# A gated cross-attention layer on one core: group loads first in SyncE's turn, rows of maxima sent by GpSimd, maxima eight groups of tiles ahead

## The chip, the cores and the metric

One core of one Trainium2 chip. The metric is device time in microseconds (us) of one execution of the whole program, as a median over runs.

## The reference, cut to what matters

Everything is float32. Four sequences of 512 tokens, width 256, 16 heads of 16.

```python
q = split_heads(layernorm(x) @ Wq.T + bq);  k, v = the same from ctx_1024
scores = einsum('bhqd,bhkd->bhqk', q, k) / 4
attn   = softmax(scores, axis=-1)
x = x + tanh(g_xattn) * (merge_heads(attn @ v) @ Wo.T + bo)
# then: a mixture of 8 experts, 2 per token, and a shared gated MLP
h = layernorm(x);  x = x + tanh(g_ffn) * (moe(h) + shared(h))
```

## The kernel before

The program has three stages. In the first, up to about 57 us, x is normalised, Q and K are projected, and each is split into a high and a low part (rows of the float32r format that TensorE multiplies), which are stored to DRAM (`q_parts`, `k_parts`). The second, from about 57 to about 335 us, is the attention loop. The third is the output projection, the router, the shared MLP and the experts.

The attention loop runs over `GROUPS` = 16 groups of `G` = 4 heads of one sequence, each in four steps `kt` over tiles of 128 keys. A step has four score products (L1608), one for each head, whose results ScalarE turns into exponentials (L806), and the products with the values of the step before (L1487), which ScalarE copies out of PSUM (L792). GpSimd adds the four steps' sums (`add_part`, L671). The transposed scores have the keys on the partitions, so the maximum over the keys can't be taken there. The kernel computes the scores a second time, with the queries on the partitions (`scores_for_max`, L1374), ahead of time, and VectorE reduces them (`two_max`, L929). The negated maxima of a group then travel: GpSimd splits them in two parts (`split_max`, L579 and L581), VectorE transposes them (`turn_max`, L937), GpSimd copies them into rows (`max_rows`, L591), and a transfer puts the rows under the Q rows of the group (`load_max`, L397). They are two more rows of the contraction of L1608, so that the maximum is subtracted in the product.

How far the maxima run ahead is `EARLY`: 28 tiles are done in the first stage by `early_max`, one at a time (L915), and `smax_schedule` then gives each step of the loop the four tiles numbered `4 * i + EARLY // TB + kt`, in fours. With 28 that is the last four tiles of group i+1 at `kt` = 0 and the first twelve of group i+2 at `kt` = 1 to 3. TensorE reaches each step's tiles after its first two scores.

`QS` and `KST` hold the Q and K rows of `NG` = 4 groups. `load_group(i)` (L387, L390) brings a group's rows from DRAM in twelve transfers of 64 KB. It may start when the scores of group i-4 are done (`st_done`).

Three more chains run in the loop. `load_sums` (L402) takes the softmax denominators of a finished group, `scale_of` (VectorE, L977) inverts them, `store_scale` (L406) and `load_scale` (L413) spread them by way of DRAM. `pack_out` (L665) moves the four heads' results from `OT` into `CTX`. `scale_context` (GpSimd, L622) multiplies two groups' results with their scales; it runs in odd turns from 5 on. `load_scale(i)` waits for `scale_context` of the pair before, since it overwrites its scales.

The order of each engine's work is written out by hand, and every queue runs in order. SyncE's turn i of the loop was `load_max(i+1)`, `load_sums(i-1)`, `store_scale(i-2)`, `load_scale(i-3)`, `load_group(i+3)`. GpSimd's turn was `split_max(i+1)`, `max_rows(i+1)`, `add_part(i-1, 3)`, `pack_out(i-1)`, `bias_x` (in the first six turns), `add_part(i, 1)`, `scale_context`, `add_part(i, 2)`. On VectorE `turn_max(i+1)` stands after the first reduction of step `kt` = 1 and `scale_of(i-2)` after that of `kt` = 2. In the last two groups a list of tail jobs (output projections, layer norm, router) is placed between the steps of TensorE and VectorE; `scale_of` of the last group comes in the last turn, ahead of the job of its step.

The last two groups do not go through `pack_out` (`TURNED` = 14): TensorE transposes their sums (`out_transpose`, L1497), which waits for GpSimd's last `add_part`.

Of the kernel before, what the change touches and what calls it, by code (L numbers as in the profile page):

```python
# [5 lines left out]
P = 128  # L6
# [3 lines left out]
F32 = mybir.dt.float32  # L10
# [5 lines left out]
def flamingo_layer(nc, x, ctxT, g_xattn, g_ffn, WqT, bq, WkT, bk, WvT, bv, WoT, bo,  # L16
# [3 lines left out]
    DK = D // H  # L20
    T = B * S
    NT = T // P
    TB = S // P
# [6 lines left out]
    G = 4  # L30
# [36 lines left out]
    with ExitStack() as stack:  # L67
# [6 lines left out]
        def sems(name, n):  # L74
            return [sem(f"{name}{i}") for i in range(n)]
# [145 lines left out]
        summed = sem("summed")  # L221
        st_done, exp_done, pv_done, sums_out = sems("st_done", 2), sem("exp_done"), sem("pv_done"), sem("sums_out")
        ot_t, rden_ready, ctx_ready = sem("ot_t"), sem("rden_ready"), sem("ctx_ready")
        ctx_in, den_in, scale_out = sems("ctx_in", 2), sems("den_in", 2), sems("scale_out", 2)
        scale_ready, scale_in, ctx_scaled = sem("scale_ready"), sems("scale_in", 2), sem("ctx_scaled")

        ct_t, wo_done, x1_ready = (sem(n) for n in ("ct_t", "wo_done", "x1_ready"))
# [34 lines left out]
            return range(UP * m, UP * (m + 1))  # L262

        STEPS = GROUPS * TB
        EARLY = 7 * G
        EARLY_J = ((0, 0, 0, 0), (0, 0, 0, 0), (2, 2, 4, 4), (4, 4, 4, 4))

        def max_tile(n):

# [76 lines left out]
        def times(i):  # L346
            return 16 * (i // 2 + 1)

        @block.sync
        def _(sp):  # L350
            sp.dma_start(CT[:, 0, :, :], ctxT[:, 0:S].rearrange("(c p) n -> p c n", p=P)).then_inc(ct_in[0], 16)
# [39 lines left out]
                                 k_scr[b, K_PART[t], rows, :].rearrange("(h r d) n -> r d h n", r=2, d=DK)[r])\  # L391
                      .then_inc(ld_group[g], 16)

            def load_max(i):
                sp.wait_ge(m_ready, TB * (i + 1))
                for part in range(2):
                    sp.dma_start(QS[i % NG][KS + part:P:HALF, :, :].bitcast(F32).rearrange("p h n -> p (h n)"),  # L397
                                 mparts[G * TB * part:G * TB * (part + 1), i % 2, :]).then_inc(m_in[i % 2], 16)

            def load_sums(i):  # L400
                sp.wait_ge(summed, (TB - 1) * (i + 1))
                sp.dma_start(DENS[:, i % 2, :], OT[i % 2][DK:P:P // G, :].rearrange("j (q n) -> j q n", n=G * TB)).then_inc(den_in[i % 2], 16)  # L402
# [28 lines left out]
            load_group(1)  # L431
            store_parts(2)
            load_group(2)
            load_max(0)
            load_group(3)
            store_parts(3)
            for i in range(GROUPS):
                if i + 1 < GROUPS:
                    load_max(i + 1)
                if 0 <= i - 1 < TURNED:  # L440
                    load_sums(i - 1)
                if 0 <= i - 2 < TURNED:
                    store_scale(i - 2)
                if 0 <= i - 3 < TURNED:
                    load_scale(i - 3)
                if i and (i + 3) % NG == 0 and i + 3 < GROUPS:
                    parts_stored((i + 3) // NG)
                if 0 < i and i + 3 < GROUPS:
                    load_group(i + 3)
                if i == GROUPS - NG + 1:  # L450
                    for t_, src in ((wgate, gate_w), (wup, up_w), (wdown, down_w)):
                        sp.dma_start(t_[:, :, :], src.rearrange("(c p) n -> p c n", p=P)).then_inc(w_in["shared"], 16)
                    sp.wait_ge(wr_zero, 1)
                    sp.dma_start(wr[:, :, 0:E], w_router.rearrange("(c p) n -> p c n", p=P)).then_inc(w_in["router"], 16)
                if i == 4:
                    parts_stored(B - 1)
                for e in EXPERTS_AT.get(i, ()):
                    load_expert(e)
                if i == GROUPS - 1:
                    sp.wait_ge(zero_ready, 3)  # L460
                    sp.dma_start(slot_x[E * CAP:ROWS, :].rearrange("(n p) d -> p n d", p=P),
                                 ZERO[:, :].unsqueeze(1).to_broadcast([P, SPARE, DT])).then_inc(zero_out, 16)
# [69 lines left out]
        def _(pool):  # L532
# [51 lines left out]
            def max_rows(i):  # L584

                pool.wait_ge(turned_max, i + 1)
                if i >= 2:
                    pool.wait_ge(m_in[i % 2], 32 * (i // 2))
                for k in range(TB):
                    at = slice(32 * k, 32 * (k + 1))  # L590
                    nc.gpsimd.tensor_copy(mparts[:, i % 2, at], mturned[at, i % 2, :]).then_inc(m_ready, 1)  # L591
                pool.wait_ge(m_ready, TB * (i + 1))

            pool.wait_ge(kones, NG)
            pool.wait_ge(w_in["small"], 64)
# [21 lines left out]
            def scale_context(n):  # L617

                for h in range(2):
                    pool.wait_ge(ctx_in[h], 16 * G * (n + 1))  # L620
                    pool.wait_ge(scale_in[h], 16 * (n + 1))
                nc.gpsimd.tensor_tensor(CTX[:, n, :], CTX[:, n, :], SCALES, ALU.mult).then_inc(ctx_scaled, 1)  # L622

# [36 lines left out]
            def pack_out(i):  # L660

                pool.wait_ge(summed, (TB - 1) * (i + 1))
                for j in range(G):
                    at = G * DK * (i % 2) + DK * j
                    pool.dma_start(CTX[at:at + DK, i // 2, :], OT[i % 2][P // G * j:P // G * j + DK, :]).then_inc(ctx_in[i % 2], 16)  # L665

            def add_part(i, kt):

# [1 line left out]
                pool.wait_ge(summed, (TB - 1) * i + kt - 1)  # L670
                nc.gpsimd.tensor_tensor(OT[i % 2], OT[i % 2], PART[kt - 1], ALU.add).then_inc(summed, 1)  # L671

            bias_x(range(4))
            for i in range(TURNED + 1):
                split_max(i + 1)
                max_rows(i + 1)
                if i:
                    add_part(i - 1, 3)
                    pack_out(i - 1)
                if i < 6:  # L680
                    bias_x(range(4 + 2 * i, 6 + 2 * i))
                add_part(i, 1)
                if i >= 5 and i % 2:
                    scale_context((i - 5) // 2)
                if i < TURNED:
                    add_part(i, 2)
# [26 lines left out]
        def _(act):  # L713
# [69 lines left out]
            def sums_copy(n):  # L783

                i, kt = divmod(n, TB)
                act.wait_ge(pv_done, n + 1)
                if kt == 0 and 2 <= i < TURNED + 2:
                    act.wait_ge(ctx_in[i % 2], G * times(i - 2))
                    act.wait_ge(den_in[i % 2], times(i - 2))
                if kt and i:  # L790
                    act.wait_ge(summed, (TB - 1) * (i - 1) + kt)
                nc.scalar.copy(PART[kt - 1] if kt else OT[i % 2], PS[:, ring_bank("sums", n), :]).then_inc(sums_out, 1)  # L792
# [97 lines left out]
        def _(dve):  # L890
# [304 lines left out]
            for i in range(GROUPS):  # L1195
                for kt in range(TB):
                    t = smax_schedule(i, kt)
                    for h in range(2):
                        if t is not None:
                            two_max(TB * t + 2 * h)  # L1200
                        if kt == 1 and h == 0 and i + 1 < GROUPS:
                            turn_max(i + 1)
                        if kt == 2 and h == 0 and 0 <= i - 2 < TURNED:
                            scale_of(i - 2)
                        if kt == 1 and h == 0 and i > TURNED:
                            denominators(i - 1)
                        if kt == 1 and h == 1 and i > TURNED:
                            head_out(i - 1)
                    tail(TB * i + kt - TAIL)
# [645 lines left out]
```

## Time and profile before

| what | us |
|---|---|
| median of 3 runs | 553.59 (552.21 to 557.13) |
| the profiled execution | 550.5 |
| its span in the profile | 548.6 |
| TensorE busy in it | 460.8 (84% of the span) |
| VectorE, ScalarE, GpSimd busy | 314.8, 269.8, 223.9 |
| mean granted TensorE clock | 0.903 of full speed |

Busy TensorE counts weight loads and low clock as they come, so a busy share of 84% does not say how near to its peak the engine is. The loop and the stage behind it have different limits, and what a change in the loop is worth is read from the waits inside it. In a line of the timeline the bracket at the end tells how long the engine sat idle ahead of it and what ended that.

### The profile page before, as it was taken

To read this page: it belongs to the slowest core of one execution; us is meant where nothing else is said; L and a number is where in the kernel's file an instruction comes from. 1 tells how busy PE (TensorE), PEld (TensorE's weight loads), DVE (VectorE), ACT (ScalarE), POOL (GpSimd) and SP (SyncE) were. 2 spreads that over 40 slices of the span, in tenths; PEclk is the share of its full clock that TensorE was granted. 3 is DMA by queue.
4 is the path that set the end of the run, shared out by engine and by line. 5 is a ranking of instruction groups with operands and counts; after the bars stand their busy time and mean duration, and the time that the engine had idled before them with its cause. 6 is when DMAs were issued, how large, how long until landed. Compare 5 with 4: busy or idle time off the path is not lost.

```text
span 548.6 us, 8362 instructions
## 1 busy us (share of the span) xinstructions
PE 460.8 (84%) x2294; PEld 232.4 (42%) x2294; DVE 314.8 (57%) x719; ACT 269.8 (49%) x564; POOL 223.9 (41%) x345
## 2 busy tenths in 40 slices
PE   9999897768836766586359997899799999999997
PEld 7554432322312222132123453546555555555555
DVE  2958667657625644565357476574556655662375
ACT  2454487767626735565366643110246666662100
POOL 5445526656613633444145525767012332322100
PEclk9999889888768867878687998999899999999999
DMA  8699602233033223321351807713222322221651
GB/s 270 238 267 244 201 21 70 69 81 76 17 67 80 50 45 66 79 59 34 67 119 41 252 3 209 232 70 111 63 59 89 86 88 81 87 88 39 228 193 58
DMA packets 45500, 58.93 MB, mean 107 GB/s; under 512 B 12496, under 2 KB 25680, under 8 KB 45456
## 3 DMA queue, kind: packets, MB, share of 16 engines
q1 hardware_dynamic: 38864, 46.05, 30.5%
q0 software_dynamic: 4960, 10.53, 5.8%
q10 hardware_dynamic: 1632, 1.84, 1.0%
q8 instruction: 19, 0.31, 0.2%
q14 instruction: 25, 0.20, 0.1%
HBM read 36.35 MB, written 19.81 MB: 102 GB/s over the span
## 4 chain that ended last, share of the span: by engine, by line
PE 59%; issue 10%; DMA 9%; SPq 8%; DVE 6%; POOL 6%; ACT 1%; another core or an unknown queue 1%; ACTq 0%; POOLq 0%; DVEq 0%
PE PS L1652 10%; PE PS L1762 8%; PE PS L1487 6%; DMA QK<-k_parts 6%; PE PS L1665 5%; PE PS L1374 5%; PE PS L1608 4%; PE PS L1781 4%; SPq L387 4%; SPq L390 3%; PE PS L1427 3%; DVE nmax L929 3%; PE PS L1757 3%; PE PS L1534 2%; POOL R L671 2%
## 5 line engine op out<-in xcount | busy, mean ns | idle before, releaser
L929 DVE TENSOR_REDUCE nmax<-PS 128x2 f32<-128x1024 f32 x114 | 135.2, 1212 | 105.7 <-PE PS L1374 105.4
L806 ACT ACTIVATE R<-PS 128x512 f32<-128x512 f32 x256 | 135.6, 624 | 85.0 <-PE PS L1608 83.6
L1374 PE MATMUL PS<-QK 48*128 48x512 f32 x256 | 71.6, 511 | 69.0 <-DMA QK<-k_parts 68.5
L1608 PE MATMUL PS<-QK 50*128 50x512 f32 x256 | 89.2, 516 | 2.0 <-ACT R L723 1.2
L1487 PE MATMUL PS<-R 128*32 128x512 f32 x512 | 82.0, 717 | 2.8 <-ACT R L806 1.6
L1374 PEld LDWEIGHTS PS<-QK 48*128 48x128 f32 x256 | 37.1, 231 | 88.6 <-DMA QK<-k_parts 73.0
L671 POOL TENSOR_TENSOR R<-R 128x512 f32<-128x512 f32 x48 | 61.8, 1287 | 31.2 <-ACT R L792 29.4
L1608 PEld LDWEIGHTS PS<-QK 50*128 50x128 f32 x256 | 42.1, 218 | 71.5 <-issue 32.6
L708 POOL DMA_INDIRECT token_y<-R,dest x34 | 32.7, 961 | 92.1 <-DVE R L1257 90.7
L591 POOL COPY mparts<-mturned 32x32 f32<-32x32 f32 x64 | 12.8, 200 | 93.6 <-DVE mturned L937 90.8
L792 ACT COPY R<-PS 128x512 f32<-128x512 f32 x64 | 38.5, 602 | 22.1 <-PE PS L1487 21.9
L1762 PE MATMUL PS<-R 128*128 x100 | 47.3, 595 | 0.2 <-ACT R L874 0.2
L821 ACT ACTIVATE R<-PS 128x512 f32<-128x512 f32 x16 | 9.6, 597 | 71.3 <-PE PS L1652 50.0
L1652 PE MATMUL PS<-R,wup 128*128 128x512 f32 x64 | 33.6, 648 | 2.3 <-issue 2.3
L629 POOL DMA_INDIRECT slot_x<-CH,pos x32 | 31.1, 971 | 10.6 <-issue 8.4
L1295 DVE TENSOR_TENSOR R<-R,PS 128x256 f32<-128x256 f32 x34 | 14.3, 421 | 32.5 <-issue 20.0
L1652 PE MATMUL PS<-R,wgate 128*128 128x512 f32 x64 | 30.6, 595 | 1.4 <-issue 1.4
L665 POOL DMA_DIRECT2D CH<-R x56 | 27.8, 502 | 4.3 <-POOL R L671 4.2
L1665 PE MATMUL PS<-wdown,R 128*128 128x256 f32 x128 | 28.9, 380 | 0.0
L871 ACT ACTIVATE R<-PS 128x256 f32<-128x256 f32 x34 | 13.0, 383 | 30.0 <-PE PS L1762 26.2
L1665 PEld LDWEIGHTS PS<-wdown,R 128*128 128x128 f32 x128 | 24.2, 192 | 4.9 <-issue 2.0
L1781 PE MATMUL PS<-fc,R 128*128 x100 | 25.6, 380 | 0.0
(181 smaller groups left out, 628.7 us busy)
## 6 DMA issues: line engine op xcount, KB each, us to landing
QK<-q_parts SPq DMA_DIRECT2D x96, 64.0 KB, 3.2
QK<-k_parts SPq DMA_DIRECT2D x96, 64.0 KB, 3.3
k_parts<-R SPq DMA_DIRECT2D x8, 512.0 KB, 3.9
q_parts<-R SPq DMA_DIRECT2D x8, 512.0 KB, 4.7
R<-in_fc_w_dram SPq DMA_DIRECT2D x16, 256.0 KB
R<-token_y SPq DMA_DIRECT2D x4, 1024.0 KB, 9.0
R<-slot_x SPq DMA_DIRECT2D x25, 129.0 KB
fc<-in_fc_w_dram SPq DMA_DIRECT2D x16, 128.0 KB
```

Of the source, the lines that this page charges most:

```text
L671: nc.gpsimd.tensor_tensor(OT[i % 2], OT[i % 2], PART[kt - 1], ALU.add).then_inc(summed, 1)
L708: nc.gpsimd.indirect_dma_start(token_y, bass.IndirectOffsetOnAxis(ap=dest[:, j:j + 1], axis=0), YE[:, j % UN, :], None).then_inc(y_out[j % ...
L792: nc.scalar.copy(PART[kt - 1] if kt else OT[i % 2], PS[:, ring_bank("sums", n), :]).then_inc(sums_out, 1)
L806: nc.scalar.activation(PT[:, kt, j, :], PS[:, ring_bank("score", TB * i + kt, j), :], ACT.Exp).then_inc(exp_done, 1)
L929: nc.vector.tensor_reduce(nmax[:, i % 2, at:G * TB:G * TB // 2], PS[:, smax_bank(n):smax_bank(n) + 2, :], AX.X, ALU.max, negate=True).then ...
L1374: mm(PS[:, smax_bank(n), :], QS[g][at, h, qt * P:(qt + 1) * P], KST[g][at, h, :], start=True, stop=True).then_inc(smax_done[n % 2], 1)
L1487: last = mm(PS[32 * j:32 * j + VW, ring_bank("sums", n), :], VA[:, b * TB + kt, (g * G + j) * VS:(g * G + j) * VS + VW], PT[:, kt, j, :], ...
L1608: mm(PS[:, ring_bank("score", TB * i + kt, j), :], KST[g][at, h, kt * P:(kt + 1) * P], QS[g][at, h, :], start=True, stop=True).then_inc(st ...
L1652: last = mm(PS[:, gu_bank(n, k), :], w[:, d, c * P:(c + 1) * P], H2T[:, d, b * S:(b + 1) * S], start=(d == 0), stop=(d == DC - 1))
L1665: last = mm(PS[:, down_bank(b, t), half * D:(half + 1) * D], HS[:, b % 2, c, t * P:(t + 1) * P], wdown[:, c, :], start=(c == 0 and half == ...
L1762: last = mm(PS[:, 1 + u, :], XGT[:, u, c * P:(c + 1) * P], fc1[:, c, e, :], start=(c == 0), stop=(c == DC - 1))
L1781: last = mm(PS[:, 5 + u, 0:D], HET[:, u, c * P:(c + 1) * P], fc2[:, c, e, :], start=(c == 0), stop=(c == IE // P - 1))
```

## The change

SyncE's turn begins with `load_group(i+3)`. `load_max` is gone from SyncE; its two transfers are issued by GpSimd at the end of `max_rows`. `EARLY` is 32, so that the tiles of a step belong to group i+2 as a whole, and the first stage does four more single maxima. `turn_max` moves from `kt` = 1 to `kt` = 0, `scale_of` from 2 to 1. Two of the four transfers of `pack_out` go to SyncE (`pack_heads`), with a semaphore for each half. On GpSimd `add_part(i-1, 3)` comes ahead of `max_rows(i+1)`, and the first `bias_x` moves behind it.

```diff
-        EARLY = 7 * G
-        EARLY_J = ((0, 0, 0, 0), (0, 0, 0, 0), (2, 2, 4, 4), (4, 4, 4, 4))
+        EARLY = 8 * G
+        EARLY_J = ((0, 0, 0, 0), (0, 0, 0, 0), (2, 2, 4, 4), (4, 4, 6, 6))
...
+        def pack_heads(queue, i, heads, done):
+
+            for j in heads:
+                at = G * DK * (i % 2) + DK * j
+                queue.dma_start(CTX[at:at + DK, i // 2, :], OT[i % 2][P // G * j:P // G * j + DK, :]).then_inc(done[i % 2], 16)
...
-            load_max(0)
             load_group(3)
             store_parts(3)
             for i in range(GROUPS):
-                if i + 1 < GROUPS:
-                    load_max(i + 1)
+                if i and (i + 3) % NG == 0 and i + 3 < GROUPS:
+                    parts_stored((i + 3) // NG)
+                if 0 < i and i + 3 < GROUPS:
+                    load_group(i + 3)
                 if 0 <= i - 1 < TURNED:
                     load_sums(i - 1)
+                    pack_heads(sp, i - 1, (2, 3), ctx_high)
                 if 0 <= i - 2 < TURNED:
                     store_scale(i - 2)
                 if 0 <= i - 3 < TURNED:
                     load_scale(i - 3)
-                if i and (i + 3) % NG == 0 and i + 3 < GROUPS:
-                    parts_stored((i + 3) // NG)
-                if 0 < i and i + 3 < GROUPS:
-                    load_group(i + 3)
...
                 pool.wait_ge(turned_max, i + 1)
                 if i >= 2:
+                    pool.wait_ge(summed, (TB - 1) * (i - 1))
                     pool.wait_ge(m_in[i % 2], 32 * (i // 2))
                 for k in range(TB):
                     at = slice(32 * k, 32 * (k + 1))
                     nc.gpsimd.tensor_copy(mparts[:, i % 2, at], mturned[at, i % 2, :]).then_inc(m_ready, 1)
                 pool.wait_ge(m_ready, TB * (i + 1))
+                for part in range(2):
+                    pool.dma_start(QS[i % NG][KS + part:P:HALF, :, :].bitcast(F32).rearrange("p h n -> p (h n)"),
+                                 mparts[G * TB * part:G * TB * (part + 1), i % 2, :]).then_inc(m_in[i % 2], 16)
...
             def pack_out(i):
 
                 pool.wait_ge(summed, (TB - 1) * (i + 1))
-                for j in range(G):
-                    at = G * DK * (i % 2) + DK * j
-                    pool.dma_start(CTX[at:at + DK, i // 2, :], OT[i % 2][P // G * j:P // G * j + DK, :]).then_inc(ctx_in[i % 2], 16)
+                pack_heads(pool, i, (0, 1), ctx_low)
...
-            bias_x(range(4))
             for i in range(TURNED + 1):
                 split_max(i + 1)
+                if i:
+                    add_part(i - 1, 3)
                 max_rows(i + 1)
                 if i:
-                    add_part(i - 1, 3)
                     pack_out(i - 1)
+                else:
+                    bias_x(range(4))
...
-                        if kt == 1 and h == 0 and i + 1 < GROUPS:
+                        if kt == 0 and h == 0 and i + 1 < GROUPS:
                             turn_max(i + 1)
-                        if kt == 2 and h == 0 and 0 <= i - 2 < TURNED:
+                        if kt == 1 and h == 0 and 0 <= i - 2 < TURNED:
                             scale_of(i - 2)
```

## Rows read from the trace of the kernel before

**Rows 1.** The list of waits of TensorE: in total, times, longest us.

```profile
PE PS L1374 <- DMA QK<-k_parts: 68.5, 12, 8.8
```

**Rows 2.** Busy time in windows: group 1, and a cycle with the wait.

```profile
core 0: us, PE busy (x) PEld busy (x) DVE busy (x) ACT busy (x) POOL busy (x), PEclk, DMA share, GB/s
76.90:86.90 10.00, 9.97 (x70) 3.85 (x66) 9.49 (x10) 9.96 (x21) 6.28 (x13) 1.00 0.09 23
...
223.40:243.70 20.30, 12.33 (x68) 4.59 (x64) 9.66 (x11) 10.30 (x21) 8.04 (x14) 0.75 0.28 64
```

**Rows 3.** Timeline of TensorE: starts of groups 2, 10 and 14, and one wait.

```profile
86.88 0.50 PE L1608 MATMUL PS<-QK 50*128 50x512 f32 x2
...
223.45 0.50 PE L1608 MATMUL PS<-QK 50*128 50x512 f32 x2
...
234.40 0.79 PE L1374 MATMUL PS<-QK 48*128 48x512 f32 x2 [7.87 <-DMA QK<-k_parts]
...
298.36 0.50 PE L1608 MATMUL PS<-QK 50*128 50x512 f32 x2
```

**Rows 4.** The list of waits of SyncE's queue: in total, times, longest us.

```profile
SPq L397 <- POOL mparts L591: 89.8, 14, 14.3
```

**Rows 5.** Timeline of SyncE's queue, one cycle: start, us, what it issues.

```profile
217.69 1.11 SPq L397 DMA_DIRECT2D QK<-mparts  x2
219.06 0.60 SPq L402 DMA_DIRECT2D DENS<-R  x1
220.56 0.34 SPq L406 DMA_DIRECT2D o_scales<-SCALE  x1
224.49 0.56 SPq L413 DMA_DIRECT2D w_v<-o_scales  x1
225.28 0.31 SPq L387 DMA_DIRECT2D QK<-q_parts  x1
...
230.30 0.42 SPq L390 DMA_DIRECT2D QK<-k_parts  x1
```

**Rows 6.** The chain that ended last: start, us, what, at that cycle's last load.

```profile
230.30 4.06 DMA QK<-k_parts
```

**Rows 7.** Timeline of GpSimd, the first bias_x, and the cycle of rows 5.

```profile
58.89 2.78 POOL L658 TENSOR_TENSOR X<-X,tg_bo 128x256 f32<-128x256 f32 x4
...
216.69 0.98 POOL L591 COPY mparts<-mturned 32x32 f32<-32x32 f32 x4 [6.45 <-DVE mturned L937]
...
219.33 1.96 POOL L665 DMA_DIRECT2D CH<-R  x4 [0.30 <-POOL R L671]
...
223.15 1.27 POOL L622 TENSOR_TENSOR CH<-CH,w_v 128x512 f32<-128x512 f32 x1
224.39 1.29 POOL L671 TENSOR_TENSOR R<-R 128x512 f32<-128x512 f32 x1
226.75 0.20 POOL L579 CAST nmax_parts<-nmax 128x16 fp32r<-128x16 f32 x1 [1.07 <-DVE nmax L929]
227.03 0.22 POOL L581 TENSOR_TENSOR nmax_parts<-nmax,nmax_parts 128x16 f32<-128x16 f32 x1
```

**Rows 8.** Timeline of ScalarE: the copy of group 9's last sums.

```profile
226.17 0.58 ACT L792 COPY R<-PS 128x512 f32<-128x512 f32 x1
```

**Rows 9.** Timeline of VectorE: four reductions without a gap, and a transposition that waited.

```profile
221.95 4.74 DVE L929 TENSOR_REDUCE nmax<-PS 128x2 f32<-128x1024 f32 x4 [0.34 <-PE PS L1374]
...
302.18 0.21 DVE L937 STREAM_TRANSPOSE mturned<-nmax_parts 128x32 f32<-128x32 f32 x1 [0.59 <-POOL nmax_parts L581]
```

**Rows 10.** Line L665, GpSimd's 56 context transfers of 32 KB: issue to landing.

```profile
DMA to landing us min/median/max: 1.8/2.0/4.4
```

**Rows 11.** Timeline of VectorE: four single maxima at the end of the first stage.

```profile
56.73 2.48 DVE L915 TENSOR_REDUCE nmax<-PS 128x1 f32<-128x512 f32 x4 [0.56 <-PE PS L1374]
```

**Rows 12.** The last group: VectorE's timeline, the chain that ended last, TensorE's timeline.

```profile
326.93 0.25 DVE L977 RECIPROCAL SCALE<-DENS 128x16 f32<-128x16 f32 x1
...
328.78 6.50 DMA w_v<-o_scales
...
339.37 0.66 PE L1497 MATMUL PS<-ident,R 128*128 128x128 f32 x4 [3.25 <-POOL R L671]
```

More of the change, by code:

```diff
@@ L223, in flamingo_layer @@
         ot_t, rden_ready, ctx_ready = sem("ot_t"), sem("rden_ready"), sem("ctx_ready")
-        ctx_in, den_in, scale_out = sems("ctx_in", 2), sems("den_in", 2), sems("scale_out", 2)
+        ctx_low, ctx_high = sems("ctx_low", 2), sems("ctx_high", 2)
+        den_in, scale_out = sems("den_in", 2), sems("scale_out", 2)
         scale_ready, scale_in, ctx_scaled = sem("scale_ready"), sems("scale_in", 2), sem("ctx_scaled")
@@ L392, in load_group @@
                       .then_inc(ld_group[g], 16)
[L394 to L398, printed above, removed]
             def load_sums(i):
@@ L619, in scale_context @@
                 for h in range(2):
-                    pool.wait_ge(ctx_in[h], 16 * G * (n + 1))
+                    pool.wait_ge(ctx_low[h], 16 * 2 * (n + 1))
+                    pool.wait_ge(ctx_high[h], 16 * 2 * (n + 1))
                     pool.wait_ge(scale_in[h], 16 * (n + 1))
@@ L787, in sums_copy @@
                 if kt == 0 and 2 <= i < TURNED + 2:
-                    act.wait_ge(ctx_in[i % 2], G * times(i - 2))
+                    act.wait_ge(ctx_low[i % 2], 2 * times(i - 2))
+                    act.wait_ge(ctx_high[i % 2], 2 * times(i - 2))
                     act.wait_ge(den_in[i % 2], times(i - 2))
```

## The prediction

> **What bounds the kernel now.** I read the list of waits first, then busy time by stage, then the timelines of the engines over two cycles of the attention loop. The loop runs over 16 groups of 4 heads, each in four steps kt. The list of waits says that TensorE's scores for the maxima (L1374) waited 68.5 us, in 12 pieces, for the transfers that load a group's Q and K rows [rows 1]. That is the largest wait of any engine for a transfer in this loop, and TensorE is the engine on which the others wait. The windows show what a cycle would be without it: group 1, from 76.9 to 86.9, takes 10.0 us with TensorE busy 9.97, ScalarE 9.96 and VectorE 9.49, at full granted clock; a cycle with the wait takes 20.3 us at a granted clock of 0.75 [rows 2]. The TensorE rows place the wait: it falls in step kt = 1 (group 10, begun at 223.45: 7.87 us), because there the scores for the maxima reach group i+2, whose rows land only then. Group 2 begins at 86.88 and group 14 at 298.36: 12 cycles in 211.5 us, 17.6 us each [rows 3].
>
> Why the rows land late stands in SyncE's order. It waited 89.8 us for the rows of maxima that GpSimd makes [rows 4]. In one cycle its queue sends those at 217.69, the denominators at 219.06, the scales at 224.49, and only then starts the twelve loads, 225.28 to 230.30 [rows 5]. The last one lands 4.06 us after its issue [rows 6]. So a load takes 9.1 us from first issue to landing, and it starts up to 1.8 us after group 10 began, or several us into a group in the other cycles, while its space has been free since the last scores of the group before.
>
> **The change part by part.** I call the start of a group T and one cycle P, and take the offsets from group 10 (T = 223.45).
>
> *Group loads first, and rows of maxima off SyncE.* SyncE's turn i now starts with load_group(i+3), which needs only the last scores of group i-1 (about T - 0.7) and a free queue. Its other work of a turn is 12 x 0.47 = 5.6 us of load issues, 0.6 for the denominators, 0.56 for the scales, 0.34 to store them, and now two context transfers, no row shows them on SyncE, at 0.42 each like a load's issue (0.60 like the denominators' at most): 8.0 us, 8.3 at most [rows 5], below any P considered. In a turn with even i the queue is late: the turn before ended with load_scale, which waits for scale_context on GpSimd. That ran at 223.15 [rows 7], and load_scale followed at 224.49 [rows 5]; this dependence stays. So in every second cycle the loads still start at T + 1.8 and land at T + 10.9. In the other they start near T - 0.5 and land at T + 8.6.
>
> *Maxima 32 tiles ahead instead of 28.* Group i+2 is now needed at kt = 0, a step (2.5 us) earlier: at T + P + 0.35, after two scores. Against T + 10.9 that asks for P of about 10.55 in late cycles and nothing in the others. The 68.5 us wait goes, and with it the low clock that follows each piece of it.
>
> *turn_max one step earlier.* What is late next is VectorE. turn_max waits for split_max on GpSimd. Today the last reduction of a group ends a step later, and split_max starts at 226.75, with GpSimd idle before it [rows 7]. In the changed order that reduction ends about 2.4 us earlier, near T + 0.9, but GpSimd is in add_part(i-1, 2) until 224.39 + 1.29 = T + 2.2 [rows 7], since it starts those adds only behind ScalarE's copy of the sums. The split takes 0.5, so it is done at T + 2.8, while VectorE, after one more reduction, is there at T + 2.1. It waits 0.7 us per group. A wait of this kind has a row in group 14: 0.59 us [rows 9]. VectorE's own work is 8 reductions at 4.74/4 = 1.185, a transposition of 0.21 and a reciprocal of 0.25: 9.9 us [rows 9, 12]. Records overlap at their ends: group 1, which has no reciprocal, shows 9.49 busy [rows 2], so I take 9.75. With the wait it is 10.45. The reductions free the banks that TensorE fills, so this sets P in the cycles whose loads come early, and the loads set 10.55 in the others. I take P = 10.5.
>
> *Rows of maxima sent by GpSimd.* The chain is: values of (i-1, 3) at kt = 0, ScalarE's copy from 226.17 [rows 8], add_part(i-1, 3) at T + 3.4 to 4.7, four copies to 5.7 (they take 0.98), two DMA issues. No row shows GpSimd sending these; its context transfers cost 1.96 for four [rows 7], so two cost 1.0 and are out at T + 7.0. They land in 1.8, 2.0 or 4.4 us (least, median, most) [rows 10]. I take 2.0: ready at T + 9.0, 1.5 us before the next group wants them. At 4.4 it would be T + 11.4, and that would be P. GpSimd's turn is 7.5 us of work (three adds 3.9, split 0.5, copies 1.0, four issues 2.0), 8.8 with scale_context, 1.4 more in the first six turns for bias_x (2.78 for four, [rows 7]): it fits. A rule of the Trainium skill speaks against this part: in SBUF — State Buffer, § Who interferes with whom, and the warning on the "DVE blocks DMA" trap, a DMA from GpSimd's queue is starved while VectorE runs in a 2-port mode, and SyncE's queue is immune. The same section says that tensor_reduce has no such mode on trn2. By the rule alone the sum would gain nothing from this part and could lose; with its exception it stands as it is. Nearly all VectorE work in the loop is that reduction.
>
> *Half the context transfers on SyncE* takes 1.0 us of issue from GpSimd and costs 0.9 on SyncE, in slack on both. They are needed only two groups later.
>
> *Prologue.* Four more single maxima (2.48/4 = 0.62 each, [rows 11]) go ahead of group 0, on a VectorE that is nearly full there: at most 2.5 us. The first scores move by 2.0. bias_x(0..3), 2.8 us of GpSimd, moves behind the first rows of maxima, where GpSimd was idle: nothing. Bounds 0 to 3.
>
> *Tail.* scale_of(13) ran at 326.93, behind the VectorE work of a tail step; one step earlier it runs near 322. The scales landed 6.5 us after 328.78, GpSimd waited for them before scale_context, its last adds came after that, and TensorE waited 3.25 us for these at 339.37 [rows 12]. With the scales 5 us earlier, the adds follow ScalarE's copies: the 3.2 us go. Bounds 0 and 3.2.
>
> **The sum.** 12 cycles at 10.5 are 126.0 against 211.5: -85.5. Group 1 gets VectorE's wait too: +0.5. Prologue +2.0, tail -3.2. Together -86.2. The profiled execution took 550.5 us, so 464.3. It lies 3.1 under the median of the runs, 553.6; I predict 467 for the median.
>
> **The rivals.**
>
> *A. Rows of maxima late.* GpSimd's issues cost more than 0.5, or the transfers land in 4.4 us beside the group loads. For: a 4.4 occurs, and its chain now ends 1.5 us before the need. Against: median 2.0. P becomes 11.4 to 12, 12 cycles: +11 to +18, 478 to 485.
>
> *B. The load wait stays in part.* SyncE in the late turns is held beyond T + 1.8, as scale_context now stands behind more GpSimd work and the loads share the engines with more transfers. P about 13 in a mean: +30, 497. If every cycle kept half of its excess over 10.5 it would be near 14, and 509. For: the late cycle has no slack. Against: the same dependence gives T + 1.8 today, and in slack.
>
> *C. Not faster.* The new ring, from a group's first values over copy, add, rows and GpSimd's transfers to the next group's start, sets P. From T + 7.0 it must take 10.6 us to land to give back 17.6. The largest landing is 4.4. Time then 553.
>
> *D. Better than the sum.* VectorE's wait is absorbed and loads land sooner: P = 10.0, the pace of group 1, and no prologue cost: 459. I count it to the likeliest case.
>
> *E. The changed order does not free SyncE.* Then nothing moves. The wait for rows of maxima, 89.8 us, is on SyncE's own queue and leaves it, so I give this almost nothing.
>
> **How the numbers follow.** Likeliest case, D in it: 0.66, 457 to 477. A: 0.17. B: 0.13. C and E: 0.02. Something better than 457: 0.02. The range for 8 in 10 reaches over the likeliest and A: 456 to 486. A difference of about 1% is what a measurement here can tell from none. The cases give faster by over 1% 0.97, within 1% 0.02, slower 0.01.
>
> **What would show it.** Right: no load wait over 1 us at L1374, and the few that are left in even groups; group starts 10 to 10.8 us apart; granted clock 1.00 through the loop; VectorE's transposition waiting some 0.7 us for the split; mparts issues of 0.5 us on GpSimd that land in about 2; the 3.25 us wait for GpSimd's last adds gone. Wrong: waits of the scores at L1608 for rows of maxima (A), loads still starting later than 2 us after a group's start (B), or GpSimd transfers that take over 5 us (C).

## The result, and the profile after

The changed kernel takes 486.8 us (median of 4, 484.7 to 489.9) where the kernel before takes 554.9 on the same chip (median of 4): a ratio of 0.878, interval 0.871 to 0.884. The forecast was 467, range 456 to 486. The sign and most of the gain came; 20 us of it did not. The profiled execution took 489.85 us with a span of 488.1, against 550.5 and 548.6 before. The spans differ by 60.5 us where the sum said 86.2. In some executions a kernel takes 1.5% or more longer than in its fastest, at a lower mean clock: the medians below include these, the ratios do not.

TensorE's list of waits in the profile after (in total, times, longest, us):

```profile
PE PS L1567 <- issue: 6.8, 1, 6.8
...
PE PS L1613 <- DMA QK<-mparts: 6.3, 5, 2.3
...
PE PS L1379 <- DMA QK<-k_parts: 1.6, 2, 0.9
```

The wait for the group loads, 68.5 us in [rows 1], is 1.6. L1613 is the score product (L1608 before), L1379 the scores for the maxima (L1374 before). New is a wait of the scores for the rows of maxima, `mparts`. The five pieces look small, but each also holds back everything behind it. (L1567 is outside the loop, and follows below.) Starts of groups 2, 8, 9 and 10 in TensorE's timeline (start, us):

```profile
95.28 0.50 PE L1613 MATMUL PS<-QK 50*128 50x512 f32 x2
...
161.47 0.50 PE L1613 MATMUL PS<-QK 50*128 50x512 f32 x2
...
174.25 0.79 PE L1613 MATMUL PS<-QK 50*128 50x512 f32 x2 [2.19 <-DMA QK<-mparts]
...
185.40 0.50 PE L1613 MATMUL PS<-QK 50*128 50x512 f32 x2
```

Group 3 starts at 105.84. Groups 2 to 5 take 10.53 to 10.56 us each, the 10.5 of the forecast. From group 6 on they take 12.8, 11.2, 12.8 (group 8, shown), 11.2 (group 9, shown), 13.0, 12.2, 11.9 and 10.2: the longest are those of groups 6, 8 and 10, every second one. After the wait, products take 0.79 us instead of 0.50 for a while: the granted clock is 0.50 for 3.4 us there. The twelve cycles take 137.4 us, forecast 126.0, before 211.5 [rows 3].

Why every second one is long stands in two queues. SyncE's queue in the turn of group 8, then GpSimd's timeline (start, us, what):

```profile
162.36 0.58 SPq L414 DMA_DIRECT2D w_v<-o_scales  x1
163.04 0.40 SPq L394 DMA_DIRECT2D QK<-q_parts  x1
...
168.16 0.42 SPq L397 DMA_DIRECT2D QK<-k_parts  x1
...
171.99 0.31 SPq L394 DMA_DIRECT2D QK<-q_parts  x1
```

```profile
160.97 1.31 POOL L626 TENSOR_TENSOR CH<-CH,w_v 128x512 f32<-128x512 f32 x1
...
167.36 1.21 POOL L594 DMA_DIRECT2D QK<-mparts  x2 [0.30 <-POOL mparts L591]
```

`load_scale` stands last in SyncE's turn and waits for `scale_context` (160.97 + 1.31 = 162.28). So the twelve loads run from 163.04 to 168.58, and the rows of maxima leave GpSimd at 167.4 to 168.6, when the loads are still on their way; the next group's loads begin at 171.99, before the rows have landed. What that does to the rows shows in the landing of L594 by window: first a turn with early loads (rows issued at 133, the last load at 131.49), then this one (167 to 169); over all 32 it is 1.8 to 6.2.

```profile
DMA to landing us min/median/max: 2.0/2.0/2.0
...
DMA to landing us min/median/max: 3.9/5.1/6.2
```

Behind early loads they land in 2.0 us; between the late loads and those of the next group the second takes 6.2 and lands near 174.2, and group 9 starts at 174.25. SyncE's own waits name what held it (L250 is the helper that waits for `ctx_scaled`):

```profile
SPq L250 <- POOL CH L626: 20.4, 5, 4.6
```

**Where the 25.8 us went** that the sum had and the spans have not. Group 1 starts 7.7 later (84.64, before 76.91), forecast 2.0: 5.7. The first score product is 2.9 of it (60.55, before 57.63), the rest is group 0 at the lower clock shown below. Group 1: 0.2. Twelve cycles: 11.4. From group 14 to TensorE's transposition of the last sums: 41.0 before, 37.7 after, -3.3 (forecast -3.2), 0.1 better. From there to the end: 209.2 before, 217.8 after: 8.6, forecast 0. The last part is for the most part a stop that was not there before (TensorE, then VectorE):

```profile
293.19 0.48 PE L1567 MATMUL PS<-ident,LT 128*128 128x128 f32 x1 [6.82 <-issue]
...
292.84 0.29 DVE L1041 COPY LT<-PS 128x128 f32<-128x128 f32 x1 [6.78 <-remote]
```

The profile names no instruction that ended TensorE's 6.8 us, but L1567 reads `LT`, and VectorE's copy into it began only at 292.84, after VectorE itself had been idle for 6.78 us. What that copy takes from PSUM was done by 284.5 (L1560). ScalarE stood too, until 294.28. GpSimd went on issuing. What held the three engines is not in the trace ("remote" is no instruction of this core). And the first stage, in windows of 5 us (columns as in [rows 2]), of after, then of before:

```profile
65.00:70.00 5.00, 3.83 (x11) 1.89 (x9) 1.23 (x1) 2.15 (x4) 4.63 (x9) 0.50 0.65 233
...
80.00:85.00 5.00, 4.91 (x32) 1.54 (x28) 4.05 (x4) 3.95 (x9) 1.29 (x1) 0.79 0.04 12
```

```profile
65.00:70.00 5.00, 5.00 (x14) 2.23 (x17) 1.47 (x3) 0.89 (x2) 2.21 (x6) 0.50 0.89 328
...
75.00:80.00 5.00, 5.00 (x36) 1.94 (x33) 4.76 (x5) 5.00 (x11) 2.61 (x2) 1.00 0.00 0
```

Both have a stretch at half clock (0.50, that is 1.2 GHz) behind the first scores. Before it is over by 75 us, after it lasts past 80.

### The profile page after: what moved, and what is told of

The parts are those of the page before. It is cut to its first block, busy times and chain, and to the rows that moved or that the text cites. A ratio compares the mean times of both kernels' runs of the same rounds, so it can differ in the third digit from the quotient of the medians.

```text
span 488.1 us, 8383 instructions
## 1 busy us (share of the span) xinstructions
PE 451.1 (92%) x2294; PEld 230.1 (47%) x2294; DVE 314.8 (64%) x721; ACT 268.1 (55%) x564; POOL 228.8 (47%) x349
## 4 chain that ended last, share of the span: by engine, by line
PE 41%; issue 7%; POOL 2%; DVE 0%; ACT 0%; POOLq 0%; DVEq 0%
PE PS L1657 12%; PE PS L1767 9%; PE PS L1670 5%; PE PS L1786 4%; PE PS L1762 3%; PE PS L1781 2%; PE PS L1741 2%; PE PS L1749 2%; POOL R L673 1%; PE PS L1539 1%; PE PS L1549 1%; POOL rstd L615 0%; DVE X L1061 0%; POOL CH L626 0%; PE PS L1560 0%
## 5 line engine op out<-in xcount | busy, mean ns | idle before, releaser
L934 DVE TENSOR_REDUCE nmax<-PS 128x2 f32<-128x1024 f32 x112 | 132.1, 1211 | 30.7 <-PE PS L1379 30.6
L1613 PE MATMUL PS<-QK 50*128 50x512 f32 x256 | 84.5, 477 | 7.6 <-DMA QK<-mparts 6.3
L673 POOL TENSOR_TENSOR R<-R 128x512 f32<-128x512 f32 x48 | 61.7, 1285 | 58.7 <-ACT R L797 58.6
L1492 PE MATMUL PS<-R 128*32 128x512 f32 x512 | 72.4, 638 | 2.8 <-ACT R L811 1.9
L1379 PE MATMUL PS<-QK 48*128 48x512 f32 x256 | 63.2, 460 | 9.8 <-DVE nmax L934 6.2
L1613 PEld LDWEIGHTS PS<-QK 50*128 50x128 f32 x256 | 37.1, 196 | 69.4 <-ACT R L811 38.7
L797 ACT COPY R<-PS 128x512 f32<-128x512 f32 x64 | 39.0, 609 | 11.3 <-PE PS L1492 11.2
L1379 PEld LDWEIGHTS PS<-QK 48*128 48x128 f32 x256 | 29.2, 199 | 32.0 <-DVE nmax L934 18.7
L1657 PE MATMUL PS<-R,wgate 128*128 128x512 f32 x64 | 33.1, 634 | 4.0 <-issue 3.9
L1300 DVE TENSOR_TENSOR R<-R,PS 128x256 f32<-128x256 f32 x34 | 14.3, 421 | 33.2 <-issue 17.4
L1657 PE MATMUL PS<-R,wup 128*128 128x512 f32 x64 | 32.2, 628 | 0.0
L1767 PEld LDWEIGHTS PS<-R 128*128 128x128 f32 x100 | 18.7, 190 | 14.3 <-issue 13.2
L920 DVE TENSOR_REDUCE nmax<-PS 128x1 f32<-128x512 f32 x32 | 19.9, 684 | 8.3 <-PE PS L1379 8.1
```

Of the source, the lines that this page charges most:

```text
L934: nc.vector.tensor_reduce(nmax[:, i % 2, at:G * TB:G * TB // 2], PS[:, smax_bank(n):smax_bank(n) + 2, :], AX.X, ALU.max, negate=True).then ...
L1379: mm(PS[:, smax_bank(n), :], QS[g][at, h, qt * P:(qt + 1) * P], KST[g][at, h, :], start=True, stop=True).then_inc(smax_done[n % 2], 1)
L1492: last = mm(PS[32 * j:32 * j + VW, ring_bank("sums", n), :], VA[:, b * TB + kt, (g * G + j) * VS:(g * G + j) * VS + VW], PT[:, kt, j, :], ...
L1613: mm(PS[:, ring_bank("score", TB * i + kt, j), :], KST[g][at, h, kt * P:(kt + 1) * P], QS[g][at, h, :], start=True, stop=True).then_inc(st ...
L1657: last = mm(PS[:, gu_bank(n, k), :], w[:, d, c * P:(c + 1) * P], H2T[:, d, b * S:(b + 1) * S], start=(d == 0), stop=(d == DC - 1))
L1767: last = mm(PS[:, 1 + u, :], XGT[:, u, c * P:(c + 1) * P], fc1[:, c, e, :], start=(c == 0), stop=(c == DC - 1))
```

## The experiments

Three theories stood for the loop. **Late turns**: SyncE is held by `load_scale` in every second turn, the loads run late, and the rows of maxima land late beside them. **GpSimd's queue**: the rows are late because GpSimd sends them. **The split**: VectorE's 0.7 us wait for `split_max` makes 10.55 of 10.0. All runs but the last (`e11`) were on a second chip, where the kernel before takes 541 us, so ratios are compared; that of `e11` is taken for the first one again, since the kernel before takes 554.1 us there.

From here on a cycle is counted from one mark to the next: the mark of a group is the first value product behind its start (L1492), some 1.5 us after it or, where TensorE is held, more. By this mark the first profile has 10.5 to 10.6 us up to group 5, then 13.7, 10.2, 13.5, 10.7, 13.4, 11.5, 11.8 and 10.2, twelve in 137.3.

### The changed kernel again

> The changed kernel as it is, beside the others of this call. If the clock in the first stage and the stop of several engines after the attention loop (6.8 us at 286 us of the profiled execution) belong to one execution and not to the program, this one takes 465 to 480 us with the kernel before at about 541 to 555; if they are the change's own, they stand in this profile too and the ratio is 0.878 again.

464.5 us (461.1 to 478.3), ratio 0.857 [0.851, 0.863]. The cycles are much the same: 10.55 up to group 5, then 12.6, 10.4, 13.4, 11.4, 11.4, 10.1, 14.0, 11.3, twelve in 136.7 us. SyncE is held 20.0 us, five times. In this profile the clock stays at 1.00 through the first stage, and the mark of group 1 comes at 77.0 us, 9.2 earlier than in the first profile (86.2). There is no stop: from the transposition to the end it is 200.0 us, 17.8 less. With the cycles' 0.6 that is 27.6 of the 27.5 us between the two spans (488.1 and 460.6). So some 11 us of the cycles come back and belong to the program; the other two terms differ between executions or chips.

### The scales' load a turn later, ahead of what would make it wait

```diff
                     load_group(i + 3)
+                if 0 <= i - 4 < TURNED - 3:
+                    load_scale(i - 4)
...
-                if 0 <= i - 3 < TURNED:
+                if i >= GROUPS - 2:
                     load_scale(i - 3)
```

> The changed kernel with one move on SyncE's queue: load_scale of a group is issued a turn later, right behind the next group loads, so that no group load stands behind the wait for scale_context. Theory A, in the changed kernel the rows of maxima land late (waits of L1613 for them, 6.3 us in 5 pieces, cycles of 12.8 and 11.2 us from group 6 on) because in every second turn the group loads start 1.6 us after the group and share the DMA engines with them: these waits go, the cycles from group 6 on fall to the 10.55 us of groups 2 to 5, about 8 x 1.4 us = 11 us less, 476 us. Theory B, GpSimd's queue is slow by itself in these turns: the waits stay, under 2 us of difference.

455.8 us, ratio 0.845 [0.838, 0.853]. All cycles but one (12.6) are 10.4 to 10.6, twelve in 128.5. SyncE's wait for `scale_context` is 1.3 us in one piece, and TensorE's products have no wait for rows or loads left in the list. GpSimd's order is untouched, and its rows leave at the same place of the cycle. Its L596 (L594 in after), in a turn in which they were late before (group 8's, issued at 157.07):

```profile
157.07 1.21 POOL L596 DMA_DIRECT2D QK<-mparts  x2 [0.30 <-POOL mparts L593]
...
DMA to landing us min/median/max: 2.3/2.5/2.7
```

Nothing but the time of the loads (and of `load_scale` itself) was changed: in late turns they start 0.85 us ahead of the group instead of 1.6 behind it, and 6.2 became 2.7 (at most 3.6 in any of the other late turns). The late-turn theory is shown.

The cycle of 12.6 that is left is group 6's, and it is not the rows'. GpSimd's turn 5 is the only one with both a `bias_x` (1.42 us) and a `scale_context` (1.27), so the split of the maxima comes later: VectorE's transposition waits 1.18 us for it, and TensorE 1.32 for VectorE's reductions at 132.77, with the clock at 0.50 for 3.4 us behind that. The same stands in the first profile (1.15 and 1.28 us).

### Rows of maxima on SyncE again, behind the group loads

```diff
+            load_max(0)
             load_group(3)
...
+                if i + 1 < GROUPS:
+                    load_max(i + 1)
...
-                    pool.dma_start(QS[i % NG][KS + part:P:HALF, ...
```

> The changed kernel with the two transfers of the rows of maxima issued by SyncE again, behind the group loads of the turn; all else as changed. Theory A (the group loads beside them make them late): in every second turn SyncE reaches them only at T + 7.1, they land no sooner than T + 9.5 to 12, cycles 11 to 12.8 us as now, 483 to 490 us. Theory B (GpSimd's queue makes them late): they land in 2 to 3 us, cycles about 10.6 us, 476 us.

462.2 us, ratio 0.854 [0.847, 0.862]; the changed kernel has 0.857. TensorE still waits for the rows, 5.7 us in 5 pieces, and the long cycles stay (13.2, 11.5, 11.8, 11.6). SyncE reaches the rows behind its loads, at T + 6.9 to 7.3 in late turns (T is the group's start) instead of GpSimd's T + 5.9. Taking them from GpSimd's queue does not remove the waits: that queue is not the cause. The first profile says the same of the context transfers in the late turn shown: from GpSimd (issued at 169.1) and from SyncE (169.9) the slowest take 7.0 and 7.2 us. The twelve cycles took 131.7, so SyncE is if anything the better sender; it was also held less by `scale_context` (7.2 us in all).

### The split ahead of the last add

```diff
+            split_max(1)
             for i in range(TURNED + 1):
-                split_max(i + 1)
...
                 if i < TURNED:
+                    split_max(i + 2)
                     add_part(i, 2)
```

> The changed kernel with one move on GpSimd: split_max of the next group is ahead of add_part(i, 2) instead of behind it. Theory C, the reason of the prediction, VectorE's wait for the split sets the cycle where nothing else does: the transposition no longer waits (7.0 us in 10 pieces now), groups 2 to 5 fall from 10.55 to about 10.0 us a cycle; from group 6 on the rows of maxima still land late, so that the gain is about 3 us in all, 484 us. Rival D, the 10.55 us are TensorE's or ScalarE's own pace: groups 2 to 5 stay at 10.5 and the time at 487.

466.4 us, ratio 0.861 [0.851, 0.870]: no gain in time. But the cycles of groups 1 to 5 fell from 10.55 to 9.9 to 10.0, and the late ones rose (13.4, 13.3, 12.0): a faster loop only runs into the late loads sooner. The wait for rows rose to 9.8 us in 4 pieces.

### Both edits

The edit of the scales' load and that of the split together.

> The changed kernel with both moves: load_scale a turn later (as in e1_scale_late) and split_max ahead of add_part(i, 2) (as in e5_split_first). Theory A and C together: no waits for rows of maxima, no wait of VectorE for the split, every cycle about 10.0 us, so 12 x 0.55 = 6.6 us under e1_scale_late: a ratio of 0.83 to the kernel before. Rival G: with the shorter cycle the rows of maxima are late again (they land at T + 9.4 at the median of 2.4 us), cycles stay at 10.5.

454.75 us (453.3 to 455.3), ratio 0.841 [0.837, 0.845]. All cycles are 10.0 but group 6's, 10.5: twelve in 120.5 us. This is the pace of group 1 before [rows 2]; in a window of 119.95 us over them TensorE is busy 118.96 and ScalarE 119.00. In group 6, with the split ahead of the add, VectorE's wait is 0.50 us. The loop is then full. The ratio is hardly below that of the scales' edit alone, since here the first stage had the low clock (0.50 from 65 to 75 us); the loop alone is 8.0 us shorter.

### Group loads first, and nothing else (on the kernel before)

```diff
             for i in range(GROUPS):
+                if i and (i + 3) % NG == 0 and i + 3 < GROUPS:
+                    parts_stored((i + 3) // NG)
+                if 0 < i and i + 3 < GROUPS:
+                    load_group(i + 3)
                 if i + 1 < GROUPS:
                     load_max(i + 1)
...
-                if 0 < i and i + 3 < GROUPS:
-                    load_group(i + 3)
```

> The kernel before with one part of the change alone: the group loads are first in SyncE's turn, ahead of the rows of maxima, which stay on SyncE; 28 tiles ahead, turn_max at kt = 1. Theory E, the order of the loads alone carries the gain: no waits for loads, the rows of maxima go out behind the loads at T + 5.6, and at T + 8.4 in every second turn; cycles of 10.0 and 11.2 us, prologue as before, about 475 us. Rival F, the parts need each other: rows of maxima behind the loads land after the next group's start, cycles of 12.5 us, 490 to 500 us.

475.4 us, ratio 0.877 [0.871, 0.884]. Of the 14.3% that the change gives on this chip, 12.3% come from this alone. Up to group 5 its cycles are 10.0 us (one 10.3), shorter than the changed kernel's; then 17.2, 16.4, 16.2 and 15.2 in every second one, with waits for the rows of 22.1 us in 4 pieces, the longest 6.2. The tail's wait for GpSimd's last adds, 2.8 us, is there, as in [rows 12].

### 28 tiles ahead instead of 32

```diff
-        EARLY = 8 * G
+        EARLY = 7 * G
...
-                        if kt == 0 and h == 0 and i + 1 < GROUPS:
+                        if kt == 1 and h == 0 and i + 1 < GROUPS:
                             turn_max(i + 1)
```

> The changed kernel with the maxima 28 tiles ahead again and turn_max at kt = 1; the order of the queues, GpSimd's transfers and scale_of as changed. Theory H, the four more tiles bring nothing, because a group load that starts with the group has 2.5 us to spare without them, and turn_max one step earlier costs the wait for the split: cycles of 10.0 us up to group 6 in place of 10.55, then rows of maxima late in every second turn as now; 2 to 5 us less than after_again. Rival I, the step earlier is needed for the rows of maxima: they go out 2 us later, wait at every group start, cycles of 11.5 us from the start, 8 us more than after_again.

468.7 us, ratio 0.864 [0.857, 0.870]. Early cycles 10.0 to 10.1, three late ones of 14.1 to 14.4 (changed kernel 12.6 to 14.0); twelve in 137.8 instead of 136.7. The two nearly cancel; a difference of 1.1 us is less than the loop of one program differs by between profiles (136.7 to 140.8, see below).

### The step of scale_of undone

`scale_of` at `kt` = 2 again.

> The changed kernel with scale_of at kt = 2 again. The prediction gave 3.2 us to this part, all of it in the last group: TensorE's wait for GpSimd's last sums (3.25 us at L1497 in the kernel before, none in the changed one) comes back, 3 us more than after_again; the loop's cycles do not change. Rival: the scales are on time anyway in the changed kernel, no wait, no difference.

473.3 us (465.6 to 473.6). TensorE's wait for GpSimd's last adds is back with 3.3 us, the size of [rows 12], and no early cycle grew by more than 0.1 us for it (twelve in 134.7): the tail's term is shown. Most of the difference in time to 464.5 is not this step: group 1 was 7.8 us later here, at low clock.

### All context transfers on GpSimd

```diff
                     load_sums(i - 1)
-                    pack_heads(sp, i - 1, (2, 3), ctx_high)
...
                 pack_heads(pool, i, (0, 1), ctx_low)
+                pack_heads(pool, i, (2, 3), ctx_high)
```

> The changed kernel with all four context transfers back on GpSimd. By the prediction's step this part of the change is worth nothing: about 1.0 us per turn goes back to GpSimd (four issues of 0.49 instead of two) behind the rows of maxima, which are sent ahead of them, and SyncE's turn is 0.9 shorter; time within 0.5% of the changed kernel, 461 to 467. The rival says that the shorter turn of SyncE lets the loads of the late turns start earlier: that can't be, if they are held by the wait for the scales' space, so cycles of 12.8 in every second turn stay. If GpSimd's queue were the limit, the split of the maxima would be later, VectorE's wait for it over 1 us per group and the early cycles 11 us instead of 10.55.

473.7 us, ratio 0.874 [0.868, 0.881] against 0.857: 2% slower where the forecast's step said nothing. Of the 15.5 us between the profiles' spans, 5.6 stand ahead of group 1 (0.50 for 14 us in the first stage) and are not this edit's. The twelve cycles took 146.5, 9.8 more. SyncE's list of waits and a stretch of GpSimd's timeline show part of why:

```profile
SPq L250 <- POOL CH L625: 31.7, 5, 7.3
```

```profile
157.24 1.99 POOL L354 DMA_DIRECT2D CH<-R  x4
...
160.54 1.30 POOL L625 TENSOR_TENSOR CH<-CH,w_v 128x512 f32<-128x512 f32 x1
```

The four issues stand ahead of `scale_context`, and SyncE is held for 31.7 us instead of 20.0, 2.3 more per late turn (31.7 - 20.0, over five). About half of that is SyncE's own: without its two issues (1.19 us) it comes to the wait sooner. The loads of the late turns start 1.6 to 3.2 us behind the group here, 1.6 to 2.3 in the changed kernel again. In the turns of groups 9, 11 and 13 GpSimd sends the rows at T + 7.1 to 8.7 instead of T + 5.9 to 7.4. So this part of the change is worth some 10 us of the loop, against my expectation that nothing would move; how the 9.8 divide between later loads and later rows is not shown.

### The extra maxima placed otherwise

```diff
-        EARLY_J = (..., (2, 2, 4, 4), (4, 4, 6, 6))
+        EARLY_J = (..., (2, 2, 6, 6), (4, 4, 4, 4))
```

Once on the changed kernel, once with the two edits.

> The changed kernel with only the other spread of the extra maxima. The late-turn theory gives the loop unchanged: cycles of 10.55 up to group 5, then 11.2 and 12.8 in turn, and waits of the scores for the rows of maxima of 5 to 7 us in all. The time is that of the changed kernel on the same chip, 461 to 466, if the extra maxima's place is of no account; some 8 us less in the executions that would otherwise have had the low clock ahead of the loop, if it is.

> The changed kernel with the scales' load ahead of the turn's other work, the split ahead of the last add (the two edits that together gave cycles of 10.0 us), and the four extra single maxima of the first stage spread otherwise: steps of 2, 2, 6, 6 and then 4, 4, 4, 4 instead of 2, 2, 4, 4 and then 4, 4, 6, 6, so that the last projections ahead of the loop are not stretched by two more maxima each. If the place of the extra maxima lets the clock fall ahead of the loop (it was 0.50 from 65 to 75 us with the two edits alone), the first stage keeps 1.00, the loop's first group starts some 8 us earlier and the time is 445 to 449. If the place of the maxima has no part in it, the low clock comes in some executions whatever the spread, and the time is 453 to 456 in those.

474.5 us, ratio 0.875 [0.869, 0.880], and 456.1 us, ratio 0.8425 [0.839, 0.846] (with the usual spread 0.8408). No gain: the clock in the first stage fell to 0.50 from 65 to 80 us in both profiles, and group 1 was later than in any other (its mark at 87.8, against 77 with the clock kept). Part of that is again a landing: GpSimd sent group 0's rows of maxima at 58.7 and 58.0, against 54.2 in the changed kernel again, they took up to 4.7 us beside the loads of group 3, and TensorE was idle for 3.2 us ahead of its first score product (64.28 and 63.62). The loop of the first of the two has the instructions of the changed kernel's and took 140.8 us, against 136.7 and 137.3: that is how far one loop differs between profiles. What makes the clock fall is not found. It stayed at 1.00 through 60 to 85 us in some profiles (the changed kernel again) and fell in others with the same instructions up to that point (both edits), behind the same gaps of TensorE.

### 28 tiles with the scales' load moved

The edits of the 28 tiles and of the scales' load together, on the first chip.

> The changed kernel with the scales' load ahead of the turn's other work (which alone gave cycles of 10.55 us throughout) and with 28 tiles of maxima ahead instead of 32, the transposition back at step 1. With 28 tiles alone the early cycles were 10.0 to 10.1, and the late ones 14.2 to 14.4. If the late turns were the whole trouble there too, all cycles are now 10.0 to 10.1, no wait for rows of maxima over 1 us is left, and the time is that of the kernel with the two edits, 454 to 457, or 2 us less for the four single maxima that the first stage is spared: then the eight groups of tiles ahead and the earlier transposition have no part in the gain once the loads are early. If the rows of maxima, made a step later, need the step that 32 tiles gave them, they are late in every turn: cycles near 11 us and 465 to 470.

462.6 us beside 554.1 for the kernel before there: 0.837 [0.832, 0.841], the lowest ratio of all, with that of the two edits inside reach. The cycles are 10.1 throughout (twelve in 121.2), and TensorE's products wait 0.5 us for rows in all (its weight loads 11.0 us in 12 pieces, which the cycles don't show). Once the loads are early, the eight groups of tiles ahead and the earlier transposition have no share in the gain; the split order is then not needed either. And on this chip the stop is back:

```profile
269.52 0.47 PE L1569 MATMUL PS<-ident,LT 128*128 128x128 f32 x1 [6.83 <-issue]
```

The same instruction, 6.83 us where it was 6.82, 24 us earlier in time; VectorE's copy ahead of it was again late (6.79 us). From the transposition to the end it took 215.8 us here, 217.8 in the first profile; 200.0 to 200.7 in all profiles of the second chip but one (201.8, `scale_of` undone).

## Why the prediction was right or wrong

**What held.** The bound was read rightly: the load wait went from 68.5 to 1.6 us. The pace of turns with early loads was forecast at 10.5 and is 10.53 to 10.56, of which the edit of the split took the 0.5 away, as the step on VectorE's wait said; that wait is

```profile
L942 DVE STREAM_TRANSPOSE mturned<-nmax_parts 128x32 f32<-128x32 f32 x16 | 3.3, 207 | 7.0 <-POOL nmax_parts L580 7.0
```

7.0 us over ten turns. Late turns were foreseen with loads from T + 1.8; group 8's began at T + 1.6 (163.04 - 161.47). GpSimd was to be done with the rows' issues at T + 7.0; it was at T + 7.1 (0.60 an issue, not 0.5). The tail's -3.2 was -3.3. The Trainium skill (SBUF — State Buffer, § Who interferes with whom) exempts tensor_reduce on trn2 from the ways in which VectorE starves GpSimd's transfers; the trace agrees, with rows landing in 2.0 us while VectorE is busy for 2.48 of 2.70 us, nearly all of it reductions (from 132.8).

**What failed: the landing of the rows.** "They land in 1.8, 2.0 or 4.4 us. I take 2.0" gave T + 9.0, with 1.5 us to spare. I knew that in late turns the loads are issued until about T + 7, beside these rows, and asked only whether the loads would land in time, not what they do to a small transfer among them. The row that it was priced by came from transfers nearly all of which had at most four group loads in flight beside them; the one of GpSimd's context transfers that had ten (issued at 86.2 in the profile before) took 3.3 us. Beside the loads it is 3.9 to 6.2, above my upper bound of 4.4, so ready at T + 12.7, and P = 12.8 there. That is rival A's mechanism: it gave 11 to 18 us for the loop, and 11.4 were measured. The size is in part luck: A had 4.4 us in every cycle, and the runs have up to 6.2 in every second one. It had 0.17, and should have been the likeliest case for the four late cycles. Moving the loads alone brought 6.2 back to 2.7 and the twelve cycles to 128.5, 8 to 9 us of the 11.4. Of the 2.5 that this still has over the forecast's 126.0, 1.9 are group 6. There "it fits" failed: GpSimd's turn of 8.8 with 1.4 for `bias_x` is shorter than a cycle, but it puts the split late, and VectorE's wait is 1.2 us instead of 0.7. The Trainium skill (DMA: Bandwidth & Descriptors, § Queues, rings and completion order) says that each DMA engine takes turns between the queues that have work for it, a whole packet at a time. The 3.9 to 6.2 us are in keeping with that, but no run here shows how the engines share.

**What failed: cost nothing.** Half the context transfers were put at zero, "in slack on both". GpSimd has idle time, but not ahead of `scale_context` in a late turn, where SyncE waits for it. Without the part the loop took 9.8 us more. Since the sum took whole cycles, the number did not suffer; the reason did. The 32 tiles I took as given, and priced only that the loads are needed a step sooner; what the kernel would be without them I did not ask. With early loads they are worth nothing.

**What failed: two terms outside the loop.** The first stage was put at +2.0 for four single maxima. The first score product came at 59.3 to 60.6 us in the changed kernel and its variants with the usual spread, against 57.2 with the group loads first alone and 57.6 before: 2.1 to 3.4 later on the second chip, 2.9 on the first. But the maxima are not the whole reason. With 28 tiles, the rows sent by GpSimd, it still came at 60.55 (59.72 on the first chip), after TensorE had been idle for 2.6 us: group 0's rows, sent at 55.5 while SyncE issues the loads of group 3, took 3.8 and 4.1 us and landed at 60.46. In the kernel before, SyncE sends them ahead of these loads. That is the same failed step once more, where I had not looked for it. The rest of the stage's excess is the clock: 0.50 for 20.5 us where the kernel before has 10.2, and that varies between executions. The last stage was put at 0 and took 8.6, through a stop at one instruction that two changed kernels show on one chip, and no profile on the other. The rest of the 8.6 is not accounted for.

If 11.4, 5.7 and 8.6 are added to the 464.3 of the sum, it is 490.0, and the profiled execution took 489.85. With the loop's term alone it would have been 476.

## What to carry to other kernels

Price a small transfer by rows with the same neighbours, and where none exists, let the range reach to the landing of the large transfers issued beside it. In a queue that runs in order, a wait at the end of one turn delays the next turn's first item: look for the late turn, and move the waiting item behind the urgent one, before anything is made faster. Idle time of an engine is slack only at the place where nobody waits for what comes behind it.

## What the runs showed of the hardware

An 8 KB transfer of GpSimd landed in 2.0 us with no 64 KB load in flight (rows issued at 205.74 in the first profile) or with the last of them issued 1.4 us ahead, and in 3.9 to 6.2 with loads issued around it. In the first stage of the changed kernel TensorE's granted clock was 1.00 throughout in one profile and 0.50 for 20.5 us in another; in those of its variants with the usual spread it was at 0.50 for 0 to 17 us. With 10, 14, 17, 17 and 20.5 us of it the mark of group 1 came 4.2, 5.6, 7.0, 7.8 and 9.2 us later than with none (the last on the first chip, the others on the second); why it falls stays open. TensorE, VectorE and ScalarE stopped at the same instructions of two kernels on one chip, TensorE for 6.82 and 6.83 us, and not at all there on another; what they waited for is not in the trace, and stays open too.
